# Two adaLN layers on one core: first-layer block scores on 64 rows at a time, two blocks a step, and all orders laid out anew

## The reference

```python
qkv = x @ W_qkv.T + b_qkv                      # layer 0, 16 heads of 16 features
q, k, v = jnp.split(qkv, 3, axis=-1)
q = q * HD ** (-0.5)
# heads and blocks: (b, 16 heads, 8 blocks of 64 tokens, 64, 16)
attn = jax.nn.softmax(jnp.einsum('bhnld,bhnmd->bhnlm', qb, kb), axis=-1)
out = jnp.einsum('bhnlm,bhnmd->bhnld', attn, vb)
```

## Time and profile before

| | |
|---|---|
| median of three runs | 1942.31 us |
| profiled execution, first to last instruction | 1941.7 us |
| TensorE busy | 1911.9 us, 98% |
| VectorE, ScalarE, GpSimd busy | 56%, 47%, 36% |
| steady part, from one batch to the next | 175.8 us |

### The profile page before, as it was taken

One profiled execution on the slowest core, in us unless ns is written; L12 is line 12 of the kernel. 1 busy time (PEld: TensorE's weight loads), 2 busy tenths in 40 slices (PEclk: granted clock), 3 DMA queues, 4 the chain that ended last, 5 costly groups with the idle time before them and its releaser, 6 DMA issues.

```text
span 1941.7 us, 30308 instructions
## 1 busy us (share of the span) xinstructions
PE 1911.9 (98%) x11192; PEld 1317.8 (68%) x11192; DVE 1093.9 (56%) x2904; ACT 919.0 (47%) x1970; POOL 694.8 (36%) x769
## 2 busy tenths in 40 slices
PE   8989999999999999999999999999999999999998
PEld 5835655765575666557656655665786888888887
DVE  5767676558556746656585655577534447223221
ACT  5646666556565555655665566454334321111111
POOL 3302334334332433252343324343443433333332
PEclk9989999999999999999999999999999999999999
DMA  3020001000000100010001000050130223333333
GB/s 129 2 87 15 12 1 39 1 23 12 28 23 1 39 1 23 1 39 15 9 13 28 13 10 15 23 176 2 31 85 4 59 73 98 66 76 79 85 76 70
DMA packets 59696, 76.78 MB, mean 40 GB/s; under 512 B 7120, under 2 KB 52824, under 8 KB 59296
## 3 DMA queue, kind: packets, MB, share of 16 engines
q1 hardware_dynamic: 46448, 57.28, 8.9%
q0 software_dynamic: 12288, 16.79, 5.0%
q10 hardware_dynamic: 816, 0.79, 0.1%
HBM read 53.71 MB, written 21.00 MB: 38 GB/s over the span
## 4 chain that ended last, share of the span: by engine, by line
PE 96%; DVE 2%; ACT 1%; DMA 0%; issue 0%; POOL 0%; SPq 0%; ACTq 0%; DVEq 0%; POOLq 0%
PE bank L765 15%; PE bank L982 12%; PE bank L995 11%; PE bank L832 7%; PE bank L887 4%; PE bank L856 4%; PE bank L868 4%; PE bank L781 3%; PE bank L750 3%; PE bank L591 3%; PE bank L900 3%; PE bank L617 3%; PE bank L841 3%; PE bank L712 2%; PE bank L818 2%; PE bank L692 2%
## 5 line engine op out<-in xcount | busy, mean ns | idle before, releaser
L1232 ACT ACTIVATE h<-bank 128x512 f32<-128x512 f32 x128 | 76.3, 597 | 363.9 <-PE bank L982 352.8
L982 PE MATMUL bank<-xin,ew 128*128 128x256 f32 x1024 | 234.3, 381 | 0.0
L995 PE MATMUL bank<-ew,h 128*128 128x256 f32 x1024 | 226.7, 379 | 0.0
L1776 POOL TENSOR_TENSOR s<-s,ri 128x256 f32<-128x256 f32 (+3 forms) x128 | 160.0, 1268 | 156.5 <-DVE ri L1531 156.5
L995 PEld LDWEIGHTS bank<-ew,h 128*128 128x128 f32 x1024 | 194.2, 190 | 27.7 <-issue 1.5
L982 PEld LDWEIGHTS bank<-xin,ew 128*128 128x128 f32 x1024 | 189.5, 190 | 23.4 <-issue 0.2
L1814 POOL DMA_INDIRECT out<-y,indices x64 | 104.2, 1628 | 265.9 <-DVE y L1668 164.9
L1208 ACT ACTIVATE s<-s,mn 128x128 f32<-128x128 f32 (+3 forms) x256 | 141.0, 552 | 109.0 <-DVE mn L1524 108.9
L1509 DVE SCALAR_TENSOR_TENSOR th<-th,bank 128x384 f32<-128x384 f32 (+1 forms) x192 | 104.3, 594 | 112.0 <-ACT th L1199 110.6
L1668 DVE SCALAR_TENSOR_TENSOR y<-bank,gates,gbe 128x256 f32<-128x256 f32 x64 | 31.0, 484 | 238.5 <-PE bank L995 230.1
L832 PE MATMUL bank<-look,term 128*128 128x384 f32 (+3 forms) x512 | 152.7, 438 | 0.0
(11 more groups left out here) (320 smaller groups left out, 3641.3 us busy)
## 6 DMA issues: line engine op xcount, KB each, us to landing
ew<-L_ffn_w SPq DMA_DIRECT2D x24, 1024.0 KB
x1s<-x_scratch SPq DMA_DIRECT2D x8, 512.0 KB
out<-x1s SPq DMA_DIRECT2D x8, 512.0 KB, 2.9
xn_scratch<-n_xn SPq DMA_DIRECT2D x8, 512.0 KB, 2.9
x<-L_attn_x SPq DMA_DIRECT2D x7, 512.0 KB, 3.8
x_scratch<-x SPq DMA_DIRECT2D x7, 512.0 KB, 3.0
wqkv<-w_qkv SPq DMA_DIRECT2D x1, 3072.0 KB, 10.7
wqkv<-L_wmod SPq DMA_DIRECT2D x2, 1024.0 KB, 8.0
```

The lines of the kernel that those rows point to most:

```text
L982: mm = te.matmul(banks[i][:, g * 2 * P:(g + 1) * 2 * P], w1[:, kk, (2 * n + g) * P:(2 * n + g + 1) * P], xin[:, kk, :, :].rearrange("p h s ...
L995: mm = te.matmul(banks[i][:, 0:D], ex.h1[:, g, n * P:(n + 1) * P], w2[:, g, :], start=(g == 0), stop=(g == FC - 1))
L1776: done = g.tensor_tensor(sc, sc, b1.ri[u % 2][:, m, :].unsqueeze(2).to_broadcast([P, 2, w]), ALU.mult)
```

## The change

The first layer's scores are computed for two blocks in one step. For each block, each head group c and each half of the rows (64 rows, two strips) there is a matmul of 64 rows by 128 query columns with 128 key columns; upper and lower rows take turns and go to two different banks. The keys need two zero patterns rather than four, so `f.k` is half as large, and ScalarE writes it over all 128 rows in two instructions (a scale and a bias that are zero in the wrong strips) rather than in four of 32 rows. `s`, `mx`, `all` and `ri` hold two blocks; the exponential, the sum and the inverse are one instruction for two blocks; maximum and subtraction are one each for each half. GpSimd still multiplies block by block, but tells of both at once. Zeroing of `k0a` and `k0b` is gone; two small tables (`strip`, `row`) and the biases `bkr` are new. `HEAD`, `PERIOD` and `LAST` are laid out anew.

```diff
-PRODUCTS = {... "sc0": 1, ...}
+PRODUCTS = {... "sc0": 2, ...}
-        self.k = early(f"k0{name}", [P, KC, NBLK, NR, LB])
+        self.k = early(f"k0{name}", [P, KC, NBLK, 2, LB])
-        self.s = [sb(f"s0{name}{i}", [P, NR, KC, LB]) for i in range(2)]
+        self.s = [place(f"s0{name}{i}", [P, 2, NR, KC, LB]) for i, place in enumerate((sb, early))]
# TensorE, sc0
-            for c in range(KC):
-                mm = te.matmul(banks[i][:, c * 256:(c + 1) * 256], f.q[:, c, n, :, :].rearrange("p a l -> p (a l)"),
-                               f.k[:, c, n, :, :].rearrange("p r m -> p (r m)"), start=True, stop=True)
-            mm.then_inc(full[i], 1)
+            for blk in range(2):
+                for c in range(KC):
+                    for h, rows in enumerate(HALVES):
+                        i, nth = at[step, b, n, h]
+                        out = banks[i][:, :].rearrange("p (b r c m) -> p b r c m", b=2, r=2, c=KC)
+                        mm = te.matmul(out[:, blk, :, c, :],
+                                       f.q[rows, c, 2 * n + blk, :, :].rearrange("p a l -> p (a l)"),
+                                       f.k[rows, c, 2 * n + blk, :, :], start=True, stop=True)
+                        if (blk, c) == (1, KC - 1):
+                            mm.then_inc(full[i], 1)
# TensorE, tp0
-            te.wait_ge(f.sem["weighted0"], lap * NBLK + n + 1)
+            te.wait_ge(f.sem["weighted0"], lap * (NBLK // 2) + n // 2 + 1)
# ScalarE, kq
-            for r in range(NR):
-                rows = slice(32 * r, 32 * r + 32)
-                done = a.activation(f.k[rows, n, :, r, :], banks[i][rows, :].rearrange("p (n m) -> p n m", m=LB),
-                                    ACT.Identity, bias=b0.bk[rows, n:n + 1])
+            for r in range(2):
+                done = a.activation(f.k[:, n, :, r, :], banks[i][:, :].rearrange("p (n m) -> p n m", m=LB),
+                                    ACT.Identity, bias=b0.bkr[:, n, r:r + 1], scale=k.const.row[:, r:r + 1])
# ScalarE, sc0
+            for h in range(2):
+                i, nth = at[step, b, n, h]
+                a.wait_ge(drained[i], nth)
+            a.activation(f.s[n % 2][:, :, :, :, :], f.s[n % 2][:, :, :, :, :], ACT.Exp).then_inc(f.sem["exp0"], 1)
# VectorE, sc0: two maxima, then two subtractions
+            for h in range(2):
+                i, nth = at[step, b, n, h]
+                v.wait_ge(full[i], nth)
+                v.tensor_reduce(mx[:, h, :], banks[i][:, :].rearrange("p (g m) -> p g m", m=LB), AX.X, ALU.max
+                                ).then_inc(f.sem["mx0"], 1)
+            if n >= 2:
+                j, old = at["tp0", b, 2 * n - 3, 0]
+                v.wait_ge(full[j], old)
...
# GpSimd, wt0: two multiplications, one signal
+            for blk in range(2):
...
+            done.then_inc(f.sem["weighted0"], 1)
# GpSimd and ScalarE at the start
-    g.memset(k.first[0].k[:, :, :, :, :], 0.0).then_inc(s["setup_pool"], 1)
-                          k.first[1].k[:, :, :, :, :].rearrange("p c n r m -> p (c n r m)")):
+    g.memset(c_.strip[:, :], 1.0).then_inc(done, 1)
+    select(c_.strip[:, :], ALU.is_ge, 0.0, 0, -32, NR, 1, 13)
+    select(c_.strip[:, :], ALU.is_ge, 0.0, 31, 32, NR, -1, 14)
# the orders, three places of them
-HEAD: 0stats:0 0silu:0 1stats:0 0wqkv_load:0 0mod_load:0 0x0:0 ... 0kq:1 1mod_load:1 0v:0 0bias0:0 0setup0:0
+HEAD: 0stats:0 1stats:0 0x0:0 0silu:0 0norm:0 1x0:0 ... 1bias0:0 0wqkv_load:0 0cols:1 0mod_load:1 0setup:0 0mod_load:0
+      0feat:0 1feat:0 0setup0:0 0kq:0 0kq:1 0w0_load:0 0rows:0 0v:1 0ga0_load:0 0sc0:0 0sc0:1 ...
-HEAD: 0out0:1 0stats:1 1tp0:6 1tp0:7 1bias0:0 1pv0:2 0norm:1 1cols:1 1pv0:3 0feat:1 ... 1cn1:0 1rows:0 0cn2:2 ...
+HEAD: 0out0:1 1pv0:2 0stats:1 0norm:1 1tp0:6 1rows:0 1pv0:3 0feat:1 ... 0fin0:0 1cn3:0 1twist:0 0feat:2 ...
-PERIOD: ... +sc0:0 +sc0:1 proj:1.2 +wt0:0 +wt0:1 -turn:11 proj:1.1 +tp0:0 ...
+PERIOD: ... look:0.1 +sc0:0 +sc0:1 +v:0 -weigh:11 -attend:10 +wt0:0 +v:1 w:0.0 proj:1.3 proj:1.2 +tp0:1 ...
```

More of the change, by code:

```diff
@@ L58 @@
[L58 to L62, removed]
@@ L77 @@
+    0attend:9 0turn:10
 """
 PERIOD = """
[L82 to L95, removed]
+    proj:0.2 +stats:0 proj:0.3 proj:0.1 +feat:0 -x1_load:0 proj:0.0 +norm:0 turn_vu:0 +kq:0 +kq:1 term:0 look:0.0
@@ new lines @@
+    +ga0_load:0 look:0.1 +sc0:0 +sc0:1 +v:0 -weigh:11 -attend:10 +wt0:0 +v:1 w:0.0 proj:1.3 proj:1.2 +tp0:1 proj:1.4
+    +wt0:1 -turn:11 proj:0.4 +tp0:0 +tp0:2 +tp0:3 +pv0:0 w:0.1 -attend:11 +pv0:1 -o_out:3 su:0 sw:0 look:0.2 sc:0 +sc0:2
+    +sc0:3 -out1:0 proj:1.1 +wt0:2 turn_vu:1 -out1:1 vc:1 proj:1.0 +x0:0 -stats_t:0 +tp0:4 +wt0:3 +tp0:5 su:1 vc:0 sw:1
+    look:1.0 +pv0:2 sc:1 look:1.1 weigh:0 +tp0:7 +tp0:6 weigh:1 su:2 term:1 sw:2 look:1.2 +pv0:3 -norm_t:0 vc:2 vc:3
+    turn:0 sc:2 +bias0:0 attend:0 weigh:2 w:1.0 turn:1 +out0:0 -feat_t:0 su:3 su:4 sw:3 sw:4 sc:3 attend:1 turn:2
@@ new lines @@
+    +out0:1 proj:2.1 +stats:1 sc:4 +norm:1 -gate:0 proj:2.0 +feat:1 proj:2.2 +cn1:0 o_out:0 w:1.1 attend:2 weigh:3
+    +cn2:0 +gc:0 look:2.0 -softmax:0 look:2.1 weigh:4 +gc:1 -probs:0 +cn3:0 +gc:2 +twist:0 turn:3 +cn4:0 proj:2.3
+    turn_vu:2 +cn1:1 su:5 proj:2.4 +cn2:1 sw:5 look:2.2 w:2.0 +cn3:1 sc:5 w:2.1 term:2 +cn4:1 proj:3.1 proj:3.2 su:7
+    +cn1:2 su:6 sw:6 sw:7 attend:3 +cn2:2 turn:4 turn_vu:3 weigh:5 +cn3:2 sc:6 sc:7 weigh:6 attend:4 turn:5 proj:3.4
+    proj:3.0 +cn4:2 o_out:1 attend:5 +gate0:0 turn:6 su:8 look:3.0 weigh:7 sw:8 proj:3.3 +fin0:0 term:3 look:3.1 sc:8
@@ L96 @@
+    w:3.0 weigh:8 attend:6 turn:7 su:9 +stats:2 sw:9 look:3.2 sc:9 w:3.1 attend:7 turn:8 su:10 weigh:9 sw:10 sc:10
+    +norm:2 su:11 attend:8 turn:9 weigh:10 o_out:2 sw:11 sc:11 attend:9 +feat:2 turn:10
 """
 LAST = """
-    7x0:0 7stats:0 5proj:0.0 5proj:0.1 5proj:0.4 5proj:0.3 7norm:0 7ga0_load:0 5proj:0.2 7feat:0 7bias0:0 5turn_vu:0
-    4attend:10 5term:0 5look:0.0 5look:0.1 5look:0.2 4weigh:11 7kq:0 7kq:1 5proj:1.2 4turn:11 7sc0:0 7wt0:0 7sc0:1
-    7wt0:1 5w:0.0 7v:0 4attend:11 7v:1 5w:0.1 7tp0:0 7sc0:2 7tp0:1 7sc0:3 7wt0:2 5vc:0 7wt0:3 5su:0 5turn_vu:1
@@ L239, in all_steps @@
     return order
-PRODUCTS = {"feat": KC, "kq": 2, "v": 1, "sc0": 1, "tp0": 1, "pv0": 1, "setup0": 1, "out0": 1, "gc": 1, "twist": KC,
+PRODUCTS = {"feat": KC, "kq": 2, "v": 1, "sc0": 2, "tp0": 1, "pv0": 1, "setup0": 1, "out0": 1, "gc": 1, "twist": KC,
             "cn2": 1, "cn3": 1, "cn4": 2, "fin0": NT // 2, "vc": 1, "proj": 1, "look": 2, "term": 2, "su": 2, "sc": 2, "turn": 2, "turn_vu": 1, "w": 1,
@@ L309, in __init__ @@
         self.group = sb("group", [P, P // HD0])
+        self.strip = sb("strip", [P, NR])
+        self.row = sb("row", [P, 2])
         self.sign = sb("sign", [P, 1])
@@ L333, in __init__ @@
         self.bk = sb("bk", [P, KC])
+        self.bkr = sb("bkr", [P, KC, 2])
         self.bv = sb("bv", [P, KC])
@@ L1277, in vector_engine @@
                 v.tensor_scalar(b0.bqp[:, c, :], c_.parity[:, :], b0.bq[:, c:c + 1], None, ALU.mult).then_inc(done, 1)
-            v.wait_ge(done, 1 + KC)
+                v.tensor_scalar(b0.bkr[:, c, :], c_.row[:, :], b0.bk[:, c:c + 1], None, ALU.mult).then_inc(done, 1)
+            v.wait_ge(done, 2 + 2 * KC)
         elif step == "silu":
```

201 lines of the change are left out of this document (101 added, 100 removed).

## The result

The changed kernel takes 1955.9 us (1954.5 to 1957.4) against 1942.2 for the kernel before on the same chip, a ratio of 1.0073 (95% interval 1.0058 to 1.0087). It is slower by 0.7%, where 1918.9 was forecast. The profiled execution is the fastest of the four; its span is 1952.9 us, 11.2 more than before.

The account below looks back on a forecast made before the run. TensorE was taken as the bound, busy 1911.9 of 1941.7 us. Span 1941.7 - 19.9 (steady scores) - 4.7 (start) + 1.2 (waits) = 1918.3, so median 1918.9 us; own range 1912 to 1925, wider range 1910 to 1930.

Parts of the forecast that it names:

- The scores' gain: Scores on TensorE: two blocks take 0.89 us instead of 1.72, 0.83 us gained a step, as in `term`.
- The drain at a change of form: TensorE entering 64-row scores steps among 128-row ones: 0.03 us a step, 1 us in all.
- The steady period: Six batches that TensorE fills: period falls by 3.3 to 172.5 us, 19.9 us gained before booked waits.
- The start: First two batches: 4.7 us gained of 6.7, 2 us lost to waits on VectorE and GpSimd.
- More waits at the start: Rival: VectorE and GpSimd bound the first two batches and the clock falls; 1925 to 1936 us, chance 0.15.
- The two-block chain: Full banks to turned weights: 7.4 us against 3.9; a wait of 0.2 us a batch, 1.2 us for six.
- My slower rival: Two-block chain ends last at `+tp0:1` in each period: 5.6 us a batch lost, about 1952 us, chance 0.06.

Follow-up runs that it names:

- e8: The kernel before with 8 one-column matmuls added in each of 32 index steps, 128 and 64 rows alternating (8 form changes a step): 2033.7 us.
- e11: The kernel before with 8 one-column matmuls added in each of 32 index steps, four of 128 rows, then four of 64 (two form changes): 2020.0 us.
- e12: e6 with three places changed in its orders, among them `pv0:0` and `pv0:1` set apart: 1935.9 us, 0.9970 of the kernel before.
- e2: The kernel after with only `LAST` taken from the kernel before, mapped to two-block steps: 1944.2 us, 1.0014 of the kernel before.
- e6: e5 with the loads at the start in the sequence of the kernel before: 1946.5 us, 1.0030 of the kernel before.
- e5: e2 with a new `PERIOD` close to the old one, scores steps paired and their turnings at least 9 us behind: 1948.3 us.
- e1: The kernel after with old `HEAD`, `PERIOD` and `LAST`, each two-block step at the place of the second one-block step: 2020.8 us, 1.0416 of the kernel before.
- e9: The kernel after with the old load order and changed `PERIOD` and `LAST`, moving steps that wait in e6: 1956.2 us, 1.0074 of the kernel before.
- e7: The kernel before with 8 one-column matmuls of 128 rows added in each of 32 index steps, no form change among them: 1997.1 us.

## Why the prediction was wrong

**The scores' gain** was right as a mechanism, with its size a little off: 0.73 us a step (57.0 to 33.4 us in 32 steps) instead of 0.83. I read the earlier trace rows as if it held an entry into another tiling form. It did not, since `term` has 64-row steps on both sides there. The new steps take 0.99 (the two at 341.81, 1.98), against 0.89 for `term`: some 0.10 goes at the first matmuls, and 0.09 on leaving where the next step has another form. Ahead of 341.81 stands a 64-row step, and the 0.10 is lost all the same; why is open.

**The drain at a change of form** is the step that failed most. "0.03 us, 1 us in all" was read from that same row. The price is 0.15 to 0.20 us between full steps, five times as much or more, and 0.086 between matmuls of one column (e8, e11). It stood in the trace of the kernel before as well, in the steps whose neighbours have another form. The Trainium skill (TensorEngine Tiling (Array Packing), Key Properties) says that a change of tiling mode drains TensorE; the runs agree that a change costs time and add the price. More than the price, the **count** was wrong: I counted the scores' own entries and never went through the new orders. "All orders laid out anew" moved hundreds of steps. From the lists, neighbours of unlike form number 441 before and 592 after, while the old orders with the new scores would have 493. Of the 151 more only about 50 are the scores'. At 0.15 to 0.20 us the 151 cost 23 to 30 us by this estimate, as much as the scores' 23.5 or more. The two traces agree: from 160 us to the end, what the steps next to a change take over the same steps with like neighbours grows from 69.0 to 97.2 us, both sides counted. (The scores' own entries and exits are in both numbers.)

**The steady period** should have fallen by 3.3 us and fell by 0.5. The scores give 3.0 (7.0 to 4.0 a batch). One place of the new `PERIOD` takes 1.0 back, the turning of the normalised rows (`feat`, TensorE in order of time, kernel after):

```profile
673.74 5.32 PE L772 MATMUL bank<-hT,wqkv 128*128 128x512 f32 x12
679.33 1.65 PE L576 MATMUL bank<-ident,n_xn 128*128 128x128 f32 x8 [0.27 <-DVE n_xn L1264]
680.81 1.88 PE L772 MATMUL bank<-hT,wqkv 128*128 128x512 f32 x4
```

The two groups take 5.59 and 1.48 us; without the wait they would take 5.16 and 0.87. Three projections stand ahead of this step in the new order and five in the old, where no such wait is; in e12, with five again, it is gone. The view of waits lists only 0.27 of the 1.04 us. The remaining 1.4 fits the changes of form, which rose from 52 to 63 a period; this part is worked out from the sum, not tried.

**The last order** was no term of my sum at all: I booked no cost to it, and nearly all of the 11.2 us over the kernel before arise there. (Against the forecast, 20.0 us are missed ahead of the sixth `fin0` and 14.5 behind it.) From the sixth `fin0` to the end the kernel before takes 939.2 us and the kernel after 950.6. Changes of form rise there from 150 to 231; at 0.15 to 0.20 that is 12 to 16 us. The same sum over the steps next to a change grows there from 26.5 to 43.1 us, and in e2, with the old `LAST`, it is 29.9. So the 12.8 us between e2 and the kernel after lie at the changes (13.2), and TensorE's listed waits there are 3 us in all. That the order does it is shown (e2, 11.7 us); that the changes of form are nearly the whole of it is counted in the traces, not tried.

**The start** should have gained 4.7 us. It gained 0.4 by the first `fin0` in the two traces, which is less than executions of one `HEAD` differ by; against the other traces it is slower by some 3 us. No gain is shown. "More waits at the start" was the right rival there, with chance 0.15. Two waits of TensorE in the kernel after answer to it (columns as in the earlier trace rows):

```profile
PE bank L545 <- DMA wqkv<-L_wmod: 11.0, 1, 11.0
PE bank L719 <- ACT a1a L1141: 3.9, 1, 3.9
```

The first matmul comes at 10.96, not at 9.00 or 9.7: the loads were moved, and it now waits for its weights. With the loads put back (e6) it comes at 9.08 instead of 11.25 in e5, but the first `fin0` gains only 0.7 us of it. The feed-forward part begins at 97.12, not near 85. Between 30 and 80 us TensorE's listed waits are 2.0 for ScalarE's copy of the turned weights, 1.6 until ScalarE has written batch 1's values and 1.2 for a bank that VectorE has not yet read out, 5.4 in all with smaller ones. Only 0.2 of it is for GpSimd's weights.

**The two-block chain** was judged about right. Full banks to turned weights take, in the kernel after (all engines in order of time):

```profile
342.97 1.29 DVE L1397 TENSOR_REDUCE mx0a<-bank 128x8 f32<-128x512 f32 x2 [0.71 <-PE bank L622]
...
347.84 1.20 DVE L1413 TENSOR_REDUCE all0a<-s0a 128x16 f32<-128x1024 f32 x1
...
349.85 4.04 POOL L1738 TENSOR_TENSOR s0a<-s0a,ri0a 128x512 f32<-128x512 f32 x4
```

That is 1.20 for the sum (1.25 taken) and 1.06 for the exponential (1.1 taken). GpSimd begins at 349.85 only, 6.9 us behind the first maxima, since the second scores step's vector work and the other layer's work on GpSimd stand in front. In the kernel after no wait for it is left in the periods, because the new orders leave 10.5 us between the scores at 341.81 and the turning at 352.33. My slower rival (1952, chance 0.06) gave nearly the time that was measured, but by a place that does not wait, so its nearness is chance. Its mechanism is real all the same: with the old places it costs 12 us a batch (e1), twice my 5.6.

**The sum.** Forecast to the sixth `fin0`: -4.7 at the start and -3.1 in each of five batches, -20.2; measured -0.2. Forecast behind it: -3.1; measured +11.4. The bounds were made for each edit by itself and held no term for the new order as a whole, so 1930 as upper end was too low.

## What to carry to other kernels

When a change lays an order out anew, count what the order itself costs before costing the edit: how often neighbouring matmuls differ in tiling form (0.15 to 0.20 us each here), and how long each producer has till its reader. A step made twice as coarse kept its throughput here but nearly doubled its latency (3.9 to 7.4 us by the sum of its parts); it needs its readers moved back, and its single buffers' readers kept apart. Where TensorE looks 99.8% busy, compare starts, not busy time: many gaps under 0.3 us were inside it here.

## What the runs showed of the hardware

- A change between 128-row, 64-row and 64-output-column matmuls costs 0.086 us between matmuls of one column. At the boundaries of steps it costs 0.09 on leaving and 0.05 to 0.10 on entering (four instructions of 512 columns: 1.72, 1.82 and 1.92 us).
- Row halves overlap nearly fully in turns (1.98 us for two steps against 3.77; `term` takes 0.89 for what is 1.79 on full rows without changes), and partly even when issued one half after the other (2.72).
- The granted clock fell for a while behind waits of 1.27 and 2.57 us at 550.5 and 555.0 (0.72 in that window of e9's slowest execution), and a period with 1.7 us more of waits became 4.2 us longer. It also stood at 0.97 to 0.98 over the last 750 us in e8 and e11 with no wait over 0.3 us, and at 1.00 in e7; the cause is open.
